# A third buffer and earlier loads for the decay rows of a gated linear attention, and its state products moved ahead of its key products

## The reference: two layers, each attention plus experts

```python
x = x + _L0_attn_ref(layernorm(x), ...) + _L0_ffn_ref(layernorm(x), ...)   # softmax attention, 16 heads
x = x + _L1_attn_ref(layernorm(x), ...) + _L1_ffn_ref(layernorm(x), ...)   # gated linear attention, 8 heads of 32
```

```python
def step(M, inp):
    q_t, k_t, v_t, f_t, g_t, o_t = inp
    M = M * f_t[..., None, None] + g_t[..., None, None] * scale * (k_t[..., :, None] * v_t[..., None, :])
    y_t = jnp.einsum('bhd,bhde->bhe', q_t, M) * o_t[..., None]
    return (M, y_t)
```

## Time and profile before

| | before |
|---|---|
| runs, us | 1610.04, 1613.28, 1602.04; median 1610.04 |
| profiled execution, us | 1610.12, of which the span from first to last instruction 1608.4 |
| mean granted TensorE clock of the span | 0.983 |
| second attention, first to last weigh | 850.4 to 1080.9 us, 32 turns |

### The profile page before, as it was taken

How to read it: one execution, slowest core, us unless ns; L and a number is a source line. 1 busy time by engine, 2 the same in 40 slices (tenths; PEclk the granted TensorE clock), 3 DMA queues, 4 the chain that set the end, 5 groups by cost and what they waited for, 6 DMA issues and landing times.

```text
span 1608.4 us, 32511 instructions
## 1 busy us (share of the span) xinstructions
PE 1526.2 (95%) x10874; PEld 1173.1 (73%) x10874; DVE 849.1 (53%) x2400; ACT 748.9 (47%) x1953; POOL 701.2 (44%) x815
## 2 busy tenths in 40 slices
PE   5888999999999999999988899989999999999997
PEld 3445545555558999997655666769999999999996
DVE  5776898888713444442587988864322123223230
ACT  4665555555641333333566666535343343433432
POOL 3232326667523555554700477832333333333331
PEclk9999999999999999999998999999999999999999
DMA  8544344555225444445432379648333333333331
GB/s 268 137 123 107 94 100 83 109 111 91 62 95 178 115 113 115 111 113 168 152 94 69 106 185 162 131 67 283 56 60 50 50 56 53 60 54 56 60 53 20
DMA packets 155835, 167.60 MB, mean 104 GB/s; under 512 B 84992, under 2 KB 132988, under 8 KB 153628
## 3 DMA queue, kind: packets, MB, share of 16 engines
q1 hardware_dynamic: 131132, 128.15, 32.4%
q0 software_dynamic: 24544, 37.38, 10.8%
HBM read 104.10 MB, written 44.45 MB: 92 GB/s over the span
## 4 chain that ended last, share of the span: by engine, by line
PE 79%; DVE 9%; DMA 4%; issue 3%; ACT 2%; SPq 1%; POOL 0%; DVEq 0%; ACTq 0%; POOLq 0%
PE PS L1686 23%; PE PS L1704 23%; PE PS L1543 4%; PE PS L1507 3%; PE PS L1528 3%; PE PS L1479 3%; PE PS L1660 2%; PE PS L1797 2%; PE PS L1614 2%; DVE PS L2009 2%; DMA arena<-FD 2%; PE PS L1569 2%; PE PS L1489 2%; PE PS L1809 1%; SPq L719 1%
## 5 line engine op out<-in xcount | busy, mean ns | idle before, releaser
L1686 PEld LDWEIGHTS PS<-arena 128*128 128x128 f32 x3408 | 398.0, 192 | 11.4
L1686 PE MATMUL PS<-arena 128*128 128x128 f32 x3408 | 404.4, 275 | 0.0
L1704 PE MATMUL PS<-arena 128*128 x1704 | 392.4, 379 | 0.0
L1704 PEld LDWEIGHTS PS<-arena 128*128 128x128 f32 x1704 | 311.9, 190 | 40.2 <-issue 0.2
L2009 DVE CUSTOM_DVE_ANT_0 PS<-PS,arena 128x512 f32<-128x512 f32 (+3 forms) x512 | 235.4, 522 | 49.3 <-PE PS L1507 48.6
L1007 POOL DMA_INDIRECT out<-arena x71 | 111.5, 1571 | 299.8 <-ACT arena L1298 277.1
L1288 ACT ACTIVATE arena<-PS,arena 128x128 f32<-128x128 f32 x568 | 162.3, 369 | 134.6 <-PE PS L1686 134.6
L2262 DVE COPY arena<-arena 128x8 f32 x71 | 12.3, 174 | 352.3 <-ACT arena L1288 333.7
L1298 ACT ACTIVATE arena<-PS,arena 128x256 f32<-128x256 f32 x142 | 67.4, 475 | 255.8 <-PE PS L1706 177.6
L993 POOL DMA_INDIRECT arena<-XN,arena x142 | 143.5, 1010 | 91.9 <-issue 35.4
L1202 ACT ACTIVATE arena<-PS 128x512 f32<-128x512 f32 (+1 forms) x256 | 166.6, 703 | 31.7 <-PE PS L1528 30.5
(11 more groups left out here) (248 smaller groups left out, 2005.4 us busy)
## 6 DMA issues: line engine op xcount, KB each, us to landing
arena<-FD SPq DMA_DIRECT2D x32, 512.0 KB
SPL<-arena SPq DMA_DIRECT2D x32, 384.0 KB, 2.7
arena<-SPL SPq DMA_DIRECT2D x64, 192.0 KB, 3.7
XN<-arena SPq DMA_DIRECT2D x16, 512.0 KB, 3.2
arena<-SPL SPq DMA_DIRECT2D x64, 128.0 KB, 3.7
arena<-SUM SPq DMA_DIRECT2D x16, 512.0 KB, 6.4
arena<-in_w SPq DMA_DIRECT2D x16, 512.0 KB
arena<-in_w SPq DMA_DIRECT2D x8, 1024.0 KB, 16.8
```

The lines of the kernel that those rows point to most:

```text
L1686: ins = pe.matmul(o, m.now[i % 2][:, c * F + 128 * f:c * F + 128 * f + 128], m.xt[i % 2][:, 128 * c:128 * c + 128], start=(c == 0), stop=( ...
L1704: ins = pe.matmul(to, m.hT[i % len(m.hT)][:, 128 * c:128 * c + 128], m.WD[:, bass.ds(e * (nf * 256) + c * 256, 256)], start=(c == 0), stop ...
```

## The change: three buffers from tile 10 on, loads three turns ahead, state products first

A third buffer `FB[2]` of 1024 columns is laid over the room that the second layer's routing uses. Tiles below 10 keep the two buffers; from tile 10 on the buffers are taken in a ring of three, (n + 1) % 3, and tile 31 uses buffer 0. Turn 8 issues the loads of rows 10 and 11, later turns that of row n + 3. The load of row 10 waits for the routing's last step (r_pos) in place of a weigh; from row 11 on a load waits for the weigh of the tile three before it, that of row 31 for the tile two before it. Since `FB[2]` covers it, the slot table's rows move to the room of LF, and POOL's first gathers of the second experts' rows also wait for the weigh of tile 28.

On PE the state products move out of `update` into `keys`, ahead of the key products; the key products of tiles 8 and up no longer start their accumulation themselves (start is set by the first state product, which writes the same bank).

```diff
             if kind == "route":
...
-            elif 0 <= n + ahead < NT and not (kind in ("decay", "decay_load") and n + ahead < 2):
+            elif kind == "decay_load":
+                out += [(kind, k) for k in ([n + 2] if n < 8 else [10, 11] if n == 8 else [n + 3]) if 2 <= k < NT]
+            elif 0 <= n + ahead < NT and not (kind == "decay" and n + ahead < 2):
                 out.append((kind, n + ahead))
...
-            r.SL = view(two, 256) if layer else view(carve(256), 256)
+            r.SL = LF.rearrange("p i h -> p (i h)") if layer else view(carve(256), 256)
...
+        FB.append(view(low_end, 1024))
+        assert low_end + 1024 <= min(route1_end, wu1)
...
-        f_in = [sem(f"f_in{n}") for n in range(2)]
+        f_in = [sem(f"f_in{n}") for n in range(3)]
...
+        def ring(n):
+            return n % 2 if n < 10 else (n + 1) % 3 if n < NT - 1 else 0
+
+        def ring_uses(n):
+            return sum(1 for k in range(n + 1) if ring(k) == ring(n))
...
-                if n >= 2:
-                    sp.wait_ge(w_put, n - 1)
-                sp.dma_start(FB[n % 2], FD[i:i + 1, :].to_broadcast([128, 1024])).then_inc(f_in[n % 2], 16)
+                if n == 10:
+                    sp.wait_ge(r_pos, 2)
+                elif n >= 2:
+                    sp.wait_ge(w_put, n - 1 if n < 10 or n == NT - 1 else n - 2)
+                sp.dma_start(FB[ring(n)], FD[i:i + 1, :].to_broadcast([128, 1024])).then_inc(f_in[ring(n)], 16)
...
             def first_rows(layer):
                 pool.wait_ge(slot_put, layer + 1)
+                if layer:
+                    pool.wait_ge(w_put, NT - 3)
...
                 pe.wait_ge(vp_put, n + 1)
+                if n >= NB:
+                    pe.wait_ge(qet_put, n - NB + 1)
+                    for g in range(2):
+                        pe.matmul(ps(7, 128 * g, 128 * g + 128), MST[:, ORDER1[n] // 4, g, :], QET2[par][:, 128 * g:128 * g + 128], start=(g == 0), stop=False, skip_group_check=True)
                 if n < NST:
                     pe.wait_ge(kd_put, n + 1)
...
-                            ins = pe.matmul(PS[32 * j:32 * j + 32, 7, o:o + 32], KD2[par][:, 32 * h:32 * h + 32], VP2[par][:, 32 * h:32 * h + 32], start=True, stop=True, skip_group_check=True)
+                            ins = pe.matmul(PS[32 * j:32 * j + 32, 7, o:o + 32], KD2[par][:, 32 * h:32 * h + 32], VP2[par][:, 32 * h:32 * h + 32], start=(n < NB), stop=True, skip_group_check=True)
                     ins.then_inc(dm_made)

             def update(n):

-                b, par = ORDER1[n] // 4, n % 2
-                if n >= NB:
-                    pe.wait_ge(qet_put, n - NB + 1)
-                    for g in range(2):
-                        pe.matmul(ps(7, 128 * g, 128 * g + 128), MST[:, b, g, :], QET2[par][:, 128 * g:128 * g + 128], start=(g == 0), stop=False, skip_group_check=True)
+                par = n % 2
                 pe.wait_ge(w_put, n + 1)
...
-                dve.wait_ge(f_in[n % 2], 16 * (n // 2 + 1))
+                dve.wait_ge(f_in[ring(n)], 16 * ring_uses(n))
...
-                dve.tensor_tensor_scan(FB[n % 2], FB[n % 2], ID8, 0.0, ALU.mult, ALU.add).then_inc(scanned)
+                dve.tensor_tensor_scan(FB[ring(n)], FB[ring(n)], ID8, 0.0, ALU.mult, ALU.add).then_inc(scanned)
```

More of the change, by code:

```diff
@@ L2418, in affinity @@
                     dve.wait_ge(y_made, n)
-                dve.tensor_tensor(WT.rearrange("p g (j n) -> p g j n", j=4), PS[:, 2:6, 0:256].rearrange("p j (g n) -> p g j n", g=2), FB[n % 2].rearrange("p (g j n) -> p g j n", g=2, j=4), ALU.mult).then_inc(w_put)
+                dve.tensor_tensor(WT.rearrange("p g (j n) -> p g j n", j=4), PS[:, 2:6, 0:256].rearrange("p j (g n) -> p g j n", g=2), FB[ring(n)].rearrange("p (g j n) -> p g j n", g=2, j=4), ALU.mult).then_inc(w_put)
             def update(n):
```

## The result

| | before | after |
|---|---|---|
| median of 9 runs each, us | 1609.01 | 1598.04 |
| lowest to highest, us | 1602.04 to 1613.28 | 1595.61 to 1599.64 |
| profiled execution (span), us | 1610.12 (1608.4) | 1598.56 (1596.8) |
| weigh of tile 8 to weigh of tile 30, us | 160.65 | 150.53 |

The ratio is 0.9934, 95% interval 0.9918 to 0.9950; by the medians it is 11.0 us faster, where 13.9 were forecast.

The account below looks back on a forecast made before the run. PE was taken to set the pace in the second attention, with late decay-row loads sometimes in its place. 1610.1 - 8.5 (loads) - 5.4 (order) = 1596.2 us; own range 1591 to 1602, 8-in-10 range 1590 to 1605.

Parts of the forecast that it names:

- What bounds the kernel: Second attention: PE's matmuls set the pace, now and then a load of decay rows; load waits cost 8.5 us.
- Loads three turns ahead: Decay-row loads in the second attention: lead grows from one turn to two, all land in time, saving 8.5 us.
- the half clock near the end: Clock of 0.50 from 1062 to 1066 us: goes once PE no longer stops, counted inside the 8.5 us.
- row 31: Load of row 31, still one turn ahead as before: costed at nothing, at most 4.9 us plus the clock.
- the wait for r_pos: Wait of row 10's load for the routing's last step: over by then, costs nothing.
- State products first: PE's order in tiles 8 to 23: key products add 0.12 instead of 0.46 us, turn 6.70 instead of 7.04, saving 5.4 us.
- the one on cover: Shorter turn: DVE's wait shrinks from 0.63 to 0.29 us, POOL's from 0.53 to 0.19, so PE stays the bound.
- The change of mode: PE's tiling modes: three changes before value products become one; two gaps of 0.17 us give the same 0.34 a turn.
- The order gives nothing: Rival on PE's order: the 0.46 us is the key products' own work, only loads count; 1601.6 us, chance 0.17.
- The ring is full: Rival on loads: transfers are short, not lead; late rows stay late, only the order pays; 1604.7 us, chance 0.12.
- Loads hold each other up: Rival on loads: two under way at once slow each other and set the turn; 1657 us, chance 0.04.
- It doesn't do what it says: Rival: third buffer held back by its r_pos wait, or a load by a weigh as late as before; 1610, chance 0.02.

Follow-up runs that it names:

- e1: The change's buffers and loads with PE's order of before (state products still in `update`); 1601.46 us, ratio 0.9954.
- e7: The kernel before, unchanged, measured and profiled a second time; 1607.55 us, ratio 1.0009.
- e5: The changed kernel with two scatters a turn instead of three in turns 10 to 24, the 15 left over moved to turns 25 to 31; 1610.60 us, ratio 1.0024.
- e4: The changed kernel again, unchanged; 1597.97 us, ratio 0.9929.
- e2: The kernel before with only the state products moved into `keys`, two buffers and loads as before; 1607.75 us, ratio 0.9998.
- e10: The changed kernel again, unchanged, beside two versions with paced scatters on one chip; 1599.40 us, ratio 0.9959.
- e6: The changed kernel with one scatter in turn 8 instead of three, and three in turn 29 instead of one; 1598.89 us, ratio 0.9941.
- e12: The kernel of e9 again, beside the changed kernel on one chip; 1593.16 us, ratio 0.9917.
- e9: The changed kernel with two scatters in turns 8 and 9, three in turn 29, and the scan waiting for project_out in turns 26 to 29; 1594.97 us, ratio 0.9888.

## Why the prediction was right, and where its sizes were off

**What bounds the kernel.** Right: PE sets the pace, and the loads' waits were on the path.

**Loads three turns ahead.** The mechanism was right in each sign named: the scan's waits are gone (12.5 us to none), the half clock near the end with them, row 31 and the wait for r_pos cost nothing. The size, 8.5 us, came out as 5.3 by e1's medians; its interval, 4.3 to 10.4, holds 8.5 too. The profiles give two reasons for less. The 8.5 was read from one execution whose second profile came out 3.0 us shorter from tile 8 to tile 30 (e7). And under the waits for loads lay late signals of PE, 1.6 us in turns 26 and 28 of e1, which the first profile didn't show.

**State products first.** "The key products add 0.12 in place of 0.46, and a turn becomes 7.04 - 0.34 = 6.70 us" was right for PE: from weight load to weight load it is 0.34 less, and with the scatter out of the way a turn is 7.05 - 6.72 = 0.33 shorter (e5). The term, 5.4 us, was mis-sized: it measured 3.5 by the medians (e4 against e1), and the profiles agree, 153.89 - 150.51 = 3.4 from tile 8 to tile 30. The failing step is the one on cover: "DVE's wait ahead of the weigh shrinks to 0.29, and POOL's wait of 0.53 us for the sums to 0.19. Both stay positive, so PE stays the bound." DVE's 0.29 was right (0.30 in e5). POOL's wait stayed at 0.53, as its input comes from the early part of the turn, which didn't move. What mattered was not POOL's idle time but what POOL does at the moment to which PE's signal moves: the end of its third scatter. With that scatter there a turn is 6.80 to 6.83 us, without it 6.72, so about 0.1 us in each of 15 turns.

**The change of mode.** The tiling page of the Trainium skill (TensorEngine Tiling (Array Packing), section Key Properties) has a change of mode drain the array; an estimate of two gaps of 0.17 gave the same 0.34, and e5's 0.33 agrees. That the price fits is luck. Between the groups of the earlier trace rows the weight loads stand idle for 0.17, 0.04 and 0.12 us at the three changes of mode; after the change the one left, ahead of L1887, has 0.11, and the loads of the value products start 0.10 ahead of the end of those of the key products. The sum falls by about a third of a microsecond, but no run shows 0.17 as the price of one change.

**Rivals.** *The order gives nothing:* its reason, that the 0.46 us is the key products' own work, is refuted in both kernels, as the turns get shorter in each. Its outcome, no gain, came about without the third buffer (e2), which the prediction didn't foresee; it added the parts as if they were independent. *The ring is full:* refuted; the DMA engines are as busy as before (share 1.02 from 978 to 1000) and no load is late. *Loads hold each other up:* refuted in the same way. *It doesn't do what it says:* refuted.

**The sum.** 13.9 forecast, 11.0 measured, and 8.8 and 7.3 when the kernel was measured again (e4, e10): the forecast was above all three. From tile 8 to tile 30 the miss is 3.8 us, 2.0 in turns 10 to 24 and 1.8 in turns 26 and 28. Turn 8, ahead of that stretch, lost another 7.71 - 6.46 = 1.25 against the first profile, for which the prediction has no term. That the two profiled executions still lie 11.6 us apart is partly luck: the first weigh came 2.7 us earlier (847.68 in place of 850.42), with the same program ahead of it.

## What to carry to other kernels

A load's lead and the length of a turn are one account: shortening the turn shortens the lead, so an edit that saves work can pay nothing while the loads are late, and its value then shows only beside the edit that makes them early. When work is moved to an earlier moment, look at what every other engine does at that moment, also at those that have idle time in the turn. And read a stall's price from more than one execution: the waits of one profile hid a second loss, and were larger than the next profile's.

## What the runs showed of the hardware

A scatter issued by POOL (one indirect transfer of 128 rows, 0.96 to 1.0 us by itself) that runs up to the end of the value products or over it goes with a late sight of PE's signal. In turn 15 of the changed kernel ACT's copy starts 0.54 us behind the products' end in place of 0.07. In turn 26 it starts 0.42 us behind the scatter's end, and there DVE is late too: the affinity ends at 1035.51, and the weigh starts at 1036.48, where 0.06 us passes between the two in turn 27. In all 19 such turns of the changed kernel's first profile the copy starts 0.34 to 0.64 us behind the end of the last scatter. When the scatter went (15 turns of e5, turn 8 of e6), the delay went; when it moved (turn 9 of e6), the delay moved; and when it ended earlier (turns 26 and 28 of e12), the delay shrank from about 1.4 to 0.4 and the turn got short. Against it stands the first profile of the kernel before, with scatters over that end in five turns and no delay, and turn 21 of e9. By which path the one reaches the other, and what else it takes, no run shows.

A scatter that starts while DVE runs its scan ends only behind the scan. In turn 15 of the changed kernel the scan runs until 955.72 + 2.28 = 958.00, and the scatter begun at 956.39 ends at 958.77, having taken 2.38 us; the one begun ahead of the scan takes 1.02. It is the same in every turn of every profile here: a scatter begun under a scan ends 0.76 to 0.87 us behind the scan's end, and one begun ahead of it, be it by 0.05 us, isn't held.

```profile
955.72 2.28 DVE L2426 TENSOR_TENSOR_SCAN arena<-arena 128x1024 f32<-128x1024 f32 x1
```

The SBUF page of the Trainium skill (SBUF — State Buffer, section SBUF: two separate sides) says that POOL can't write the descriptors of its transfers while certain operations of DVE hold the port that the two share; the row agrees, for a scan, though that it is this port no run shows. So the third scatter's place hangs on the scan, and e9 and e12 could make turns 26 to 28 short by holding the scan back 0.42 us: the first scatter gets in ahead of it, and the one over the value products ends about 0.95 us earlier than in the changed kernel.
